# A mixture-of-experts product on TensorE: units of one expert by two token tiles become units of one token tile by two experts

## The chip, the core and the metric

The kernel runs on one core of a Trainium2 chip. The metric is the device time of one launch in microseconds; lower is better. Three runs of the kernel before gave 2796.57, 2797.51 and 2797.83 us, so the median is 2797.51 us.

## What is computed

Two transformer layers on x of shape 32 batches x 256 tokens x 256 features: cross attention, a mixture layer, a second attention without weights, and a sparse expert layer. The change touches only the mixture layer, which multiplies every token by all 12 experts, with a weight C that is zero for all but the three chosen ones:

```python
h = jax.nn.gelu(_mixture(xf, C1, W1), approximate=False)
y = _mixture(h, C2, W2) + C3 @ b2
# _mixture: for e in range(12): y = y + C[:, e:e + 1] * (inp @ W[e].T)
```

Every `inp @ W[e].T` is a 256x256 by 256x256 product for each batch; there are two mixtures (n = 0 with W1, n = 1 with W2), so 24 expert products in each of 32 batches, 768 in all.

## The kernel before, in words

All engines walk one list of pieces, `order`, that the function `pieces` sorts by hand-set places (the tables PLACES, MIX, OPENING and LAST at the head of the file). In the steady part a batch's work is spread over 40 places, and pieces of about five batches are interleaved: the attention of a later batch runs between the mixture products of an earlier one. Each engine takes from the list the pieces in which it has a part, in that order, and waits on semaphores only. Nothing is reordered at run time.

A mixture piece is `("mix", b, n, l)`, with b the batch, n the mixture and l from 0 to 11; its number is q = 24 b + 12 n + l. Tokens of a batch form two tiles t of 128 tokens; features form two blocks dt of 128.

- **TensorE** (`tensor_program`, line 1447). To keep fp32 accuracy with the fp32r type, each operand is split into a high and a low part, and a product is the sum of three terms (high by high, low by high, high by low), so 3 x 2 = 6 matmuls fill one output region. The stationary operand is a 128x128 block of tokens (`r_part`, `h_part` has the same memory), the moving one 128x256 of the expert's weights (`w_h`, `w_l`). The piece has 12 matmuls of 256 columns, six for each token tile, and fills one 512-column PSUM bank, `mixp[q % 2]`. Before it, TensorE waits until VectorE has done all adds of piece q - 2, which used the same bank. After it, `t_mix` goes up by one.
- **VectorE** (`vector_program`, line 1131; line 1125 for the first add of a tile in mixture 0). It waits for `t_mix` of the piece and does two adds, acc = psum * C + acc, of 128x256 elements: one for token tile 0, one for token tile 1. Each add waits through the semaphore `v_mix` for the add of the piece before that wrote the same tile. These two adds don't depend on each other.

Between mixture pieces TensorE does, among others: `first` (line 1347, attention scores whose row maxima VectorE takes at line 1039), `second` (1365, scores that ScalarE turns into exponentials at 854), `attn_out` (1381), transposes into the bank `misc` (1273, 1355, 1392), projections (1315, 1327, 1411), router products (1426, 1428, 1429), and the shared expert (1483, 1504, 1522). VectorE also does layer norm statistics (973 to 978, 1000), the attention's division (1057, 1062), splits into high and low parts (949, 954), `nmp` (1049, 1051) and the router's selection (1082 to 1111). The sparse experts run at the end, from about 2490 us, and have no mixture pieces.

Of the kernel before, what the change touches and what calls it, by code (L numbers as in the profile page):

```python
# [15 lines left out]
P = 128  # L16
# [234 lines left out]
def build(nc, x_in, ctx_in, ctxT_in, wqT_in, wkvT_in, woT_in, qk_cols_in, bv_cols_in, bo_in, pw_in, uT_in,  # L251
          w1T_in, w2T_in, b2_in, wgu_in, wd_in, wsgu_in, wsd_in, out_pad):
    NB, S, D = x_in.shape
    T = NB * S
    TILES = S // P
    DT = D // P
# [12 lines left out]
    NXB = 5  # L269
# [3 lines left out]
    TERMS = ((0, 0), (1, 0), (0, 1))  # L273
# [6 lines left out]
    with ctx:  # L280
# [9 lines left out]
        def sems(name, n):  # L290
# [18 lines left out]
        wmix = [[sb(f"w{n}_{p}", (P, L, DT, D), F32R) for p in "hl"] for n in (1, 2)]  # L309
# [13 lines left out]
        X = [x_mem[:, i] for i in range(NXB)]  # L323
        hid = sb("hid", (P, TILES, D))
# [36 lines left out]
        Cw = [sb(f"C{i}", (P, TILES, 3, L)) for i in range(2)]  # L361
# [51 lines left out]
        mixp, bank1, bank2 = ([mem[:, k, :] for k in range(2)] for mem in (mixp_mem, first, second))  # L413
# [47 lines left out]
        v_k, v_qt, v_q, v_ot, v_xo, v_rt, v_z, v_zd, v_C, v_mix, v_b2, v_ht, v_c3 = (  # L461
            sem(f"dve_{n}") for n in ("k", "qt", "q", "ot", "xo", "rt", "z", "zd", "C", "mix", "b2", "ht", "c3"))
# [454 lines left out]
        def vector_program(dve):  # L917
# [39 lines left out]
            for what, *a in order:  # L957
                if what == "w_mix":
                    split_lo(FIRST + a[0])
                elif what == "ln1":  # L960
                    kind, b = a
                    src = X[b % NXB]
# [16 lines left out]
                elif what == "ln2":  # L979
                    kind, b = a  # L980
                    src = X[b % NXB]
# [20 lines left out]
                elif what == "k_proj":  # L1002
                    b, = a
                    dve.wait_ge(a_k, 2 * (b + 1))
                    lo_biased(k_nat, 1, v_k)
                elif what == "c_done" and a[0] == NB - 1:
                    b, = a
# [4 lines left out]
                elif what == "q_proj":  # L1012
                    b, = a
                    dve.wait_ge(a_q, q_parts_of(job_J["A", b]))
                    lo_biased(q_nat, 0, v_q)
                elif what == "c_turn":
                    b, = a
                    dve.wait_ge(a_q, q_parts_of(job_J["C", b]))
                    lo(q_nat, v_q)
                elif what == "q_turn":  # L1020
                    b, = a
                    dve.wait_ge(a_qt, b + 1)
                    lo(a_parts, v_qt)
                elif what == "o_turn":
                    b, = a
                    dve.wait_ge(a_ot, b + 1)
                    lo(a_parts, v_ot)
                elif what == "r_turn":
                    b, = a
                    dve.wait_ge(a_rt, b + 1)  # L1030
                    lo(r_parts, v_rt)
                elif what == "h_turn":
                    b, = a
                    dve.wait_ge(a_ht, b + 1)
                    lo(h_parts, v_ht)
                elif what == "s1":
                    kind, b, J, h, u, j = a
# [5 lines left out]
                elif what == "max_rows":  # L1043
                    kind, b, J, h, u = a
# [8 lines left out]
                elif what == "out_turn":  # L1053
                    kind, b, J, h, u = a
# [10 lines left out]
                elif what == "o_proj":  # L1065
                    b, = a
# [3 lines left out]
                elif what == "r_z":  # L1070
                    b, = a
# [5 lines left out]
                elif what == "r_top":  # L1077
                    b, = a
# [34 lines left out]
                elif what == "mix":  # L1113
                    b, n, l = a
                    q = 2 * L * b + n * L + l
                    dve.wait_ge(t_mix, q + 1)
                    for t in range(TILES):
                        acc = (hid if n == 0 else X[b % NXB])[:, t, :]
                        src = mixp[q % 2][:, t * D:(t + 1) * D]
                        c = Cw[b % 2][:, t, n, l:l + 1]  # L1120
                        if n == 0 and l == 0:
                            dve.wait_ge(v_C, b + 1)
                            dve.wait_ge(t_ht, b)
                            dve.wait_ge(a_id, 1)
                            dve.e.tensor_scalar(acc, src, c, None, ALU.mult).then_inc(v_mix, 1)
                        else:
                            if l == 0:
                                dve.wait_ge(v_b2, 2 * b + t + 1)
                            else:
                                dve.wait_ge(v_mix, 2 * (q - 1) + t + 1)  # L1130
                            dve.e.scalar_tensor_tensor(acc, src, c, acc, ALU.mult, ALU.add).then_inc(v_mix, 1)  # L1131
                elif what == "b2":
                    b, = a
# [4 lines left out]
                elif what == "d_logits":  # L1138
                    b, = a
# [7 lines left out]
                elif what == "d_top":  # L1147
                    b, = a
# [29 lines left out]
                elif what == "d_pos":  # L1178
                    b, = a
# [21 lines left out]
                elif what == "d_up":  # L1201
                    b, = a
# [6 lines left out]
                elif what == "d_down":  # L1209
                    b, = a  # L1210
# [3 lines left out]
                elif what == "e_same":  # L1214
                    e, = a
# [18 lines left out]
                elif what == "e_gate":  # L1234
                    e, = a
# [4 lines left out]
                elif what == "e_down":  # L1240
                    e, = a
# [8 lines left out]
        def tensor_program(pe):  # L1250
# [26 lines left out]
            for dt in range(DT):  # L1277
                m = pe.e.matmul(misc[:, dt * 64:dt * 64 + 3 * L], pw[:, dt * P:(dt + 1) * P], uT[:, :], start=True,
                                stop=True)
# [3 lines left out]
            for dt in range(DT):  # L1283
                m = pe.e.matmul(mixp[0][0:2, 0:D], bv_cols[:, dt, :], stage[0][:, dt * D:(dt + 1) * D], start=(dt == 0),
                                stop=(dt == DT - 1))
            m.then_inc(t_bo, 1)
            pe.wait_ge(a_id, 1)
            for what, *a in order:
                if what == "q_turn":
                    b, = a  # L1290
# [3 lines left out]
                elif what == "c_turn":  # L1294
                    b, = a
# [3 lines left out]
                elif what in ("k_proj", "q_proj"):  # L1299
                    b, = a  # L1300
# [9 lines left out]
                    for c in range(2):  # L1310
                        out = misc[:, c * S:(c + 1) * S]
                        n = 0
                        for i, j in TERMS:
                            for dt in range(DT):
                                m = pe.e.matmul(out, w[j][:, dt, c * P:(c + 1) * P], x[i][:, dt, :], start=(n == 0),  # L1315
                                                stop=(n == 3 * DT - 1))
                                n += 1
                    m.then_inc(t_kp if isk else t_q, 1)
                elif what == "v_proj":
                    b, = a  # L1320
                    claim("misc", (a_v, b + 1))
                    for t in range(TILES):
                        out = misc[:, t * D:(t + 1) * D]
                        n = 0
                        for i, j in TERMS:
                            for dt in range(DT):
                                m = pe.e.matmul(out, ctx_parts[i][:, dt, t * P:(t + 1) * P], wkv[j][:, dt, D:2 * D],
                                                start=(n == 0), stop=(n == 3 * DT - 1))
                                n += 1
                    m.then_inc(t_vp, 1)  # L1330
                elif what == "s1":
                    kind, b, J, h, u, j = a
# [17 lines left out]
                elif what == "max_rows":  # L1350
                    kind, b, J, h, u = a
# [43 lines left out]
                elif what == "o_turn":  # L1395
                    b, = a
# [34 lines left out]
                elif what == "mix":  # L1431
# [8 lines left out]
                    else:  # L1440
                        pe.wait_ge(v_ht, b + 1)
                    src = r_parts if n == 0 else h_parts
                    for t in range(TILES):
                        k = 0
                        for i, j in TERMS:
                            for dt in range(DT):
                                m = pe.e.matmul(mixp[q % 2][:, t * D:(t + 1) * D], src[i][:, dt, t * P:(t + 1) * P],  # L1447
                                                wmix[n][j][:, l, dt, :], start=(k == 0), stop=(k == 3 * DT - 1))
                                k += 1
                    m.then_inc(t_mix, 1)  # L1450
                elif what == "c3":
                    b, = a
# [188 lines left out]
```

## Time and profile before

| | |
|---|---|
| median of three runs | 2797.51 us (2796.57 to 2797.83) |
| span of the profiled execution | 2796.0 us |
| TensorE matmul busy | 2627.6 us, 94% |
| TensorE weight loads busy | 2189.7 us, 78% |
| VectorE busy | 2229.3 us, 80% |
| ScalarE, GpSimd busy | 1074.1 us, 38%; 808.2 us, 29% |
| mean granted TensorE clock | 0.981 of 2.4 GHz |

The span is the time from the first to the last instruction of the one profiled execution; it is 1.5 us under the median of the runs, and no separate time of that execution was taken. Matmuls are pipelined: a matmul's recorded duration is longer than the distance to the next one's start, so the distance of starts is what a matmul costs in a row of them. Weight loads have a row of their own and overlap matmuls. In a timeline, consecutive instructions of one form are merged, with their count behind an x.

### The profile page before, as it was taken

The numbers are of one execution on the slowest core, as the hardware profiler recorded it, in microseconds if no ns is written. First come the engines' busy times: TensorE is split into PE (matmuls) and PEld (weight loads), VectorE is DVE, ScalarE is ACT, GpSimd is POOL, SyncE is SP. The second block draws the span as 40 slices with busy tenths as digits, with TensorE's granted clock in tenths as the row PEclk, the third lists the DMA queues.
The fourth block names the chain that finished last, engine by engine and source line by source line (L and its number), as shares of the span: only waits on it lengthen the run. The fifth ranks groups of instructions, "written<-read, shape, count | busy, mean of one in ns | idle before, by whom it ended". The sixth has DMA issues, their size and how long they took to land.

```text
span 2796.0 us, 59981 instructions
## 1 busy us (share of the span) xinstructions
PE 2627.6 (94%) x22949; PEld 2189.7 (78%) x22949; DVE 2229.3 (80%) x6135; ACT 1074.1 (38%) x1622; POOL 808.2 (29%) x829
## 2 busy tenths in 40 slices
PE   3899999999999999999999999999999999985999
PEld 2788788888888888888888888888888888763776
DVE  5678788888888888888888888888888888762554
ACT  3333334444434444433444444444443444322232
POOL 1000132322223222222222222322222232226444
PEclk9999999999999999999999999999999999986999
DMA  7644444444444434443444444343444343245997
GB/s 224 175 136 105 113 123 130 123 110 111 117 116 108 116 107 100 116 110 94 110 103 97 114 116 109 105 116 101 96 108 98 92 107 71 58 87 155 231 234 168
DMA packets 322210, 336.02 MB, mean 120 GB/s; under 512 B 46676, under 2 KB 302751, under 8 KB 321412
## 3 DMA queue, kind: packets, MB, share of 16 engines
q1 hardware_dynamic: 286404, 307.37, 42.4%
q0 software_dynamic: 33792, 18.52, 3.9%
q10 hardware_dynamic: 1728, 6.29, 0.7%
q8 instruction: 182, 2.98, 0.5%
q14 instruction: 104, 0.85, 0.1%
HBM read 191.65 MB, written 221.81 MB: 148 GB/s over the span
## 4 chain that ended last, share of the span: by engine, by line
PE 76%; DVE 17%; issue 3%; DMA 2%; POOL 1%; ACT 1%; SPq 1%; POOLq 0%; ACTq 0%; DVEq 0%
PE mixp L1447 34%; PE attn_out L1381 6%; DVE nm L1039 6%; PE first L1347 5%; PE second L1365 4%; DVE hid L1131 4%; PE misc L1315 3%; PE mixp L1549 3%; PE misc L1273 3%; PE misc L1483 2%; PE second L1568 2%; PE misc L1522 2%; PE misc L1392 2%; DVE xhat L1000 2%; PE first L1504 2%
## 5 line engine op out<-in xcount | busy, mean ns | idle before, releaser
L739 POOL DMA_INDIRECT expert_slots<-row_mem,sidx x512 | 507.2, 991 | 1065.1 <-PE first L1347 769.5
L854 ACT ACTIVATE exps<-second 128x1024 f32<-128x1024 f32 x512 | 525.7, 1027 | 735.8 <-PE second L1365 727.7
L1447 PE MATMUL mixp<-w_h,r_part_h 128*128 128x256 f32 x3072 | 666.8, 298 | 10.9 <-DVE hid L1131 6.1
L1039 DVE TENSOR_REDUCE nm<-first 128x4 f32<-128x1024 f32 x504 | 613.7, 1218 | 27.0 <-PE first L1347 23.6
L1447 PE MATMUL mixp<-w_h,r_part_l 128*128 128x256 f32 x3072 | 610.9, 280 | 0.0
L1447 PE MATMUL mixp<-w_l,r_part_h 128*128 128x256 f32 x3072 | 610.3, 280 | 0.0
L1447 PEld LDWEIGHTS mixp<-w_h,r_part_h 128*128 128x128 f32 x3072 | 469.0, 189 | 60.5 <-DVE hid L1131 22.2
L1447 PEld LDWEIGHTS mixp<-w_l,r_part_h 128*128 128x128 f32 x3072 | 469.7, 188 | 0.0
L1447 PEld LDWEIGHTS mixp<-w_h,r_part_l 128*128 128x128 f32 x3072 | 469.6, 188 | 0.0
L1131 DVE SCALAR_TENSOR_TENSOR x_mem<-mixp,C,x_mem 128x256 f32<-128x256 f32 x768 | 334.7, 477 | 75.4 <-PE mixp L1447 72.0
L1131 DVE SCALAR_TENSOR_TENSOR hid<-mixp,C,hid 128x256 f32<-128x256 f32 x704 | 301.5, 476 | 97.0 <-PE mixp L1447 96.8
L713 POOL TENSOR_TENSOR norm<-norm,minus_half 128x2 f32<-128x2 f32 x128 | 91.9, 718 | 699.9 <-DVE norm L978 699.9
L1381 PE MATMUL attn_out<-exps,vx 128*17 128x256 f32 x4096 | 273.7, 389 | 4.5 <-ACT exps L854 4.5
L1347 PE MATMUL first<-kst,qst 48*128 48x256 f32 x2016 | 235.8, 311 | 23.4 <-DMA qst<-q_parts 17.5
L1365 PE MATMUL second<-qst,kst 50*128 50x256 f32 x2048 | 234.9, 307 | 7.3 <-ACT exps L854 5.5
L1347 PEld LDWEIGHTS first<-kst,qst 48*128 48x128 f32 x2016 | 155.8, 188 | 75.4 <-issue 29.5
L1365 PEld LDWEIGHTS second<-qst,kst 50*128 50x128 f32 x2048 | 158.8, 189 | 61.3 <-issue 30.0
L1381 PEld LDWEIGHTS attn_out<-exps,vx 128*17 128x17 f32 x4096 | 95.2, 97 | 101.7 <-issue 24.7
L750 POOL DMA_INDIRECT out<-x_mem,sidx x64 | 99.0, 1547 | 113.6 <-DVE x_mem L1248 65.8
L861 ACT COPY out_sb<-attn_out 128x512 f32<-128x512 f32 x128 | 74.6, 583 | 101.0 <-PE attn_out L1381 98.2
L786 ACT ACTIVATE nat_h<-misc,qk_cols 128x256 fp32r<-128x256 f32 x128 | 53.7, 471 | 154.6 <-PE misc L1315 149.2
L1000 DVE TENSOR_SCALAR xhat<-x_mem,norm 128x256 f32<-128x256 f32 x192 | 93.7, 529 | 5.0 <-POOL norm L713 5.0
(236 smaller groups left out, 3585.9 us busy)
## 6 DMA issues: line engine op xcount, KB each, us to landing
kst<-k_parts SPq DMA_DIRECT2D x256, 192.0 KB, 4.0
qst<-q_parts SPq DMA_DIRECT2D x256, 192.0 KB, 4.5
q_parts<-nat_h SPq DMA_DIRECT2D x128, 256.0 KB
k_parts<-ctx_part_h SPq DMA_DIRECT2D x64, 256.0 KB, 2.5
k_parts<-nat_h SPq DMA_DIRECT2D x64, 256.0 KB, 5.6
q_parts<-nat_l SPq DMA_DIRECT2D x64, 256.0 KB
exps<-in_wgu SPq DMA_DIRECT2D x30, 384.0 KB, 4.0
expert_slots<-row_mem SPq DMA_DIRECT2D x16, 642.0 KB, 6.3
```

The lines of the kernel that those rows point to most:

```text
L713: pool.e.tensor_tensor(rstd[kind][:, :], veps[kind][:, :], minus_half[:, :], ALU.pow).then_inc(p_pow[kind], 1)
L739: pool.e.indirect_dma_start(out=slots_dram, out_offset=bass.IndirectOffsetOnAxis(ap=sidx[b % 2][:, t, k:k + 1], axis=0), in_=row[b % 2][:, ...
L750: pool.e.indirect_dma_start(out=out_pad, out_offset=bass.IndirectOffsetOnAxis(ap=eid[e % NID], axis=0), in_=ey[e % NY], in_offset=None, bo ...
L854: act.e.activation(exps[:, j % NU, :, :, :].rearrange("p k t s -> p (k t s)"), second[:, :, :].rearrange("p k s -> p (k s)"), ACT.Exp, sca ...
L1000: dve.e.tensor_scalar(dst[:, t, 0:D], src[:, t, :], mv[kind][:, t, 0:1], rstd[kind][:, t:t + 1], ALU.subtract, ALU.mult).then_inc(v_norm[k ...
L1039: dve.e.tensor_reduce(nm[u % 2][:, :, 2 * j:2 * j + 2].rearrange("p t k -> p k t"), (mixp_mem if in_mixp(b, kind, j) else first)[:, :, :]. ...
L1131: dve.e.scalar_tensor_tensor(acc, src, c, acc, ALU.mult, ALU.add).then_inc(v_mix, 1)
L1273: m = pe.e.transpose(v[:, dt, t * P:(t + 1) * P], src[:, t, dt * P:(dt + 1) * P], ident)
L1347: m = pe.e.matmul(bank[k][:, t * S:(t + 1) * S], q_st[u % 3][at, j, t * P:(t + 1) * P], k_st[u % 3][at, j, :], start=True, stop=True)
L1365: m = pe.e.matmul(bank2[k][:, s * S:(s + 1) * S], k_st[u % 3][at, j, s * P:(s + 1) * P], q_st[u % 3][at, j, :], start=True, stop=True)
L1381: m = pe.e.matmul(attn_out[r0:r0 + HD + 1, q * S:(q + 1) * S], vx[:, s, h * H // 2 + HQ * q + i, :], exps[:, (2 * q + i // 2) % NU, i % 2, ...
L1447: m = pe.e.matmul(mixp[q % 2][:, t * D:(t + 1) * D], src[i][:, dt, t * P:(t + 1) * P], wmix[n][j][:, l, dt, :], start=(k == 0), stop=(k == ...
```

## The change

The two experts 2i and 2i + 1 keep two pieces, but these divide the work the other way round. The piece with even l takes token tile 0 through both experts, the piece with odd l takes token tile 1 through both. On TensorE a piece is six matmuls; the moving operand is `wmix[n][j][:, e:e + 2, dt, :]`, two experts' 256 columns, 512 in all. On VectorE both adds of a piece write the same tile, and the second waits for the first. The list of pieces, the banks, and TensorE's waits stay.

```diff
--- before.py
+++ after.py
@@ -1114,20 +1114,24 @@
                     dve.wait_ge(t_mix, q + 1)
-                    for t in range(TILES):
-                        acc = (hid if n == 0 else X[b % NXB])[:, t, :]
-                        src = mixp[q % 2][:, t * D:(t + 1) * D]
-                        c = Cw[b % 2][:, t, n, l:l + 1]
-                        if n == 0 and l == 0:
+                    t = l % 2
+                    acc = (hid if n == 0 else X[b % NXB])[:, t, :]
+                    for i in range(2):
+                        e = l // 2 * 2 + i
+                        src = mixp[q % 2][:, i * D:(i + 1) * D]
+                        c = Cw[b % 2][:, t, n, e:e + 1]
+                        if n == 0 and e == 0:
                             dve.wait_ge(v_C, b + 1)
                             dve.wait_ge(t_ht, b)
                             dve.wait_ge(a_id, 1)
                             dve.e.tensor_scalar(acc, src, c, None, ALU.mult).then_inc(v_mix, 1)
                         else:
-                            if l == 0:
+                            if e == 0:
                                 dve.wait_ge(v_b2, 2 * b + t + 1)
+                            elif i:
+                                dve.wait_ge(v_mix, 2 * q + 1)
                             else:
-                                dve.wait_ge(v_mix, 2 * (q - 1) + t + 1)
+                                dve.wait_ge(v_mix, 2 * (q - 1))
                             dve.e.scalar_tensor_tensor(acc, src, c, acc, ALU.mult, ALU.add).then_inc(v_mix, 1)
@@ -1440,13 +1444,13 @@
                     src = r_parts if n == 0 else h_parts
-                    for t in range(TILES):
-                        k = 0
-                        for i, j in TERMS:
-                            for dt in range(DT):
-                                m = pe.e.matmul(mixp[q % 2][:, t * D:(t + 1) * D], src[i][:, dt, t * P:(t + 1) * P],
-                                                wmix[n][j][:, l, dt, :], start=(k == 0), stop=(k == 3 * DT - 1))
-                                k += 1
+                    e, t = l // 2 * 2, l % 2
+                    k = 0
+                    for i, j in TERMS:
+                        for dt in range(DT):
+                            m = pe.e.matmul(mixp[q % 2][:, 0:2 * D], src[i][:, dt, t * P:(t + 1) * P],
+                                            wmix[n][j][:, e:e + 2, dt, :], start=(k == 0), stop=(k == 3 * DT - 1))
+                            k += 1
                     m.then_inc(t_mix, 1)
```

## Rows read from the trace of the kernel before

**Rows 1.** The page: shares of the engines, chain by engine and line, two groups.
```profile
PE 2627.6 (94%) x22949; PEld 2189.7 (78%) x22949; DVE 2229.3 (80%) x6135; ACT 1074.1 (38%) x1622; POOL 808.2 (29%) x829
...
PE 76%; DVE 17%; issue 3%; DMA 2%; POOL 1%; ACT 1%; SPq 1%; POOLq 0%; ACTq 0%; DVEq 0%
PE mixp L1447 34%; PE attn_out L1381 6%; DVE nm L1039 6%; PE first L1347 5%; PE second L1365 4%; DVE hid L1131 4%; PE misc L1315 3%; PE mixp L1549 3%; PE misc L1273 3%; PE misc L1483 2%; PE second L1568 2%; PE misc L1522 2%; PE misc L1392 2%; DVE xhat L1000 2%; PE first L1504 2%
...
L1447 PE MATMUL mixp<-w_h,r_part_l 128*128 128x256 f32 x3072 | 610.9, 280 | 0.0
...
L1131 DVE SCALAR_TENSOR_TENSOR x_mem<-mixp,C,x_mem 128x256 f32<-128x256 f32 x768 | 334.7, 477 | 75.4 <-PE mixp L1447 72.0
```

**Rows 2.** Windows: one batch's period, and the steady part (stretch, length, busy us).
```profile
1006.60:1082.40 75.80, 74.24 (x687) 62.87 (x687) 65.60 (x180) 31.04 (x45) 21.91 (x23) 1.00 0.42 108
400.00:2200.00 1800.00, 1762.63 (x16308) 1492.53 (x16308) 1556.09 (x4236) 737.63 (x1046) 520.12 (x546) 1.00 0.43 109
```

**Rows 3.** Waits, 400 to 2200 us: us in total, times, longest us.
```profile
DVE hid L1131 <- PE mixp L1447: 72.9, 71, 1.9
...
DVE x_mem L1131 <- PE mixp L1447: 43.9, 96, 0.9
...
PE misc L1273 <- DVE ctx_o L1062: 11.9, 24, 0.5
```

**Rows 4.** The chain in order of time, 1000 to 1090 us (start, us, what).
```profile
1001.54 0.88 DVE hid L1131 x2
...
1006.59 0.53 DVE hid L1131 x2
...
1010.80 1.67 PE mixp L1447 x12
...
1027.55 0.88 DVE hid L1131 x2
...
1029.61 1.57 PE first L1504 x8
```

**Rows 5.** Timeline of TensorE, matmuls (start, us from first start to last end).
```profile
1003.30 0.40 PE L1447 MATMUL mixp<-w_h,r_part_h 128*128 128x256 f32 x2
...
1004.70 0.40 PE L1447 MATMUL mixp<-w_h,r_part_h 128*128 128x256 f32 x2
...
1039.51 0.28 PE L1355 MATMUL misc<-identr,nmp 128*16 128x128 f32 x2
```

**Rows 6.** Timeline of the sparse experts near 2652 us, and their groups by form.
```profile
2651.93 1.46 PE L1549 MATMUL mixp<-exps,xhat 128*128 128x384 f32 x4
...
2653.44 1.03 PE L1568 MATMUL second<-vx,router_mem 96*128 96x256 f32 x4
...
L1549 PE MATMUL mixp<-exps,xhat 128*128 128x384 f32 x120 | 43.7, 486 | 0.0
...
L1568 PE MATMUL second<-exps,router_mem 96*128 96x256 f32 x120 | 30.9, 379 | 0.0
```

**Rows 7.** Timeline: the first and the last of eight weight loads for the router.
```profile
1070.57 0.19 PEld L1426 LDWEIGHTS misc<-gT_both,r_part_h 128*128 128x128 f32 x1
...
1071.35 0.19 PEld L1429 LDWEIGHTS misc<-gT_both,r_part_h 128*128 128x128 f32 x1
```

**Rows 8.** Timeline of VectorE (start, us; in brackets idle before it and releaser).
```profile
1011.74 1.66 DVE L1131 SCALAR_TENSOR_TENSOR hid<-mixp,C,hid 128x256 f32<-128x256 f32 x4
...
1020.75 0.88 DVE L1131 SCALAR_TENSOR_TENSOR hid<-mixp,C,hid 128x256 f32<-128x256 f32 x2 [1.93 <-PE mixp L1447]
...
1039.19 0.18 DVE L1051 TENSOR_TENSOR nmp<-nm,nmp 128x16 fp32r<-128x16 f32 x1
...
1062.11 0.29 DVE L1193 TENSOR_TENSOR prep<-prep,pmask 128x128 f32<-128x128 f32 x1
1062.44 0.35 DVE L1196 MAX8 stop<-prep 128x8 f32<-128x64 f32 x2
...
1069.74 0.69 DVE L949 TENSOR_TENSOR r_part_l<-misc,r_part_h 128x512 fp32r<-128x512 f32 x1
```

## The prediction, written before the changed kernel was run

> **What bounds the kernel now.** I read the page first. TensorE is busy 94% of the span, VectorE 80%, and the chain that ended last is TensorE for 76% and VectorE for 17%; line 1447, the mixture, holds 34% of it alone [rows 1]. A share over the whole span hides stages, so I read windows next. In the steady part TensorE is busy 1762.6 of 1800 us; one batch takes 75.8 us, with 74.24 of TensorE and 65.60 of VectorE [rows 2]. So TensorE idles 1.56 us a batch and VectorE 10.2. The clock is at its upper level (1.00) there and plays no part. Then the waits: VectorE waits for mixture products 72.9 + 43.9 = 116.8 us over 24 batches, 4.9 us a batch; TensorE's waits for VectorE are short and regular, such as 0.5 us once a batch for `ctx_o` [rows 3]. Last the chain in order of time, which shows that a batch has two kinds of stretch. From 1001.5 to about 1015 us VectorE sets the pace: the chain runs through its adds and reaches TensorE at 1010.80 [rows 4]; it catches up only at 1020.75, where it waits 1.93 us [rows 8]. Outside that stretch TensorE is nearly always what is late, except for short visits such as the add at 1027.55 that leads to line 1504 at 1029.61 [rows 4].
>
> **TensorE's part.** The columns streamed stay the same; the number of matmuls and weight loads falls from 12 to 6 a piece. Two equal places of adjacent pieces start 1.40 us apart (1003.30, 1004.70) [rows 5], so a 256-column matmul costs 1.40 / 12 = 0.117 us. What would 512 columns cost? No fp32r matmul of that width is in the trace, so I bound it. Above: twice 0.117 = 0.235 us, and no gain. Below: the time of a weight load, since a load is still needed for each; where the moving operand has only 36 or 72 columns, eight loads start over 1071.35 - 1070.57 = 0.78 us, 0.111 us each [rows 7]. Between them I take the plain-fp32 rows. There 128 columns more cost 486 - 379 = 107 ns of duration, and a 256-column fp32r matmul lasts 280 ns, 99 less than a 256-column fp32 one [rows 1, 6]: fp32r streams a column in about half the time, so 512 fp32r columns weigh what 256 fp32 columns do. Four of those take 1.03 us, and with the last one's 0.379 us off the step is (1.03 - 0.379) / 3 = 0.217 us, with a weight load hidden behind each; the 384-column ones confirm it with (1.46 - 0.486) / 3 = 0.325 us, 0.108 more [rows 6]. So a piece costs 6 x 0.217 = 1.30 us in place of 1.41: **0.106 us less**, 0 at the upper bound, 0.74 at the lower. If the excess of a 256-column matmul over its streaming (117 - 107 = 10 ns) is paid once per matmul however wide it is, the step is 0.224 us and the gain 0.064.
>
> **VectorE's part.** It still does two adds a piece, of the same size. Before, neighbours are independent: four in a row take 1.66 us with 0.477 us for one [rows 1, 8], so they start (1.66 - 0.477) / 3 = 0.395 us apart and overlap by 0.08. After, the second add waits for the first. A dependent pair of neighbours in the trace is 1062.11 + 0.29 = 1062.40, next start 1062.44 [rows 8]: no overlap and a gap of 0.04. The second add then starts 0.477 + 0.035 = 0.51 us behind the first: **0.115 us more a piece**, 2.8 us a batch. Bounds: nothing, if the overlap survives; at the top the longer hand-off from VectorE to TensorE, 1039.19 + 0.18 = 1039.37 to 1039.51, 0.14 us [rows 5, 8], which makes 0.22. I take 0.115, as that row is the same engine waiting for itself. The Trainium skill speaks against charging this: "VectorE: DVE Perf Modes", section "The DRAIN you can't avoid", says that the next operation does not begin before the pipeline has emptied, and that a semaphore between two operations adds nothing. By that rule the charge is zero. The starts 0.395 us apart with durations of 0.477 do not agree with it.
>
> The other edits cost nothing. The first add of a piece now waits for all adds up to piece q - 2, not for the last piece's; those have left VectorE two instructions before. The waits on C, on the bias of the second mixture and TensorE's wait for piece q - 2 stay. Behind the new wait stands all of VectorE's queue: the row maxima (line 1039) that free bank `first`, the `ctx_o` and `nmp` steps that release transposes, and the adds that free `mixp`.
>
> **The sum.** Of 24 pieces a batch, I go along the stretches. In the VectorE-paced stretch the products of six pieces are not late, so their gain is lost, and six pieces' adds lie on the path: 6 x 0.115. The add before line 1504 is on the path [rows 4]. Two more hand-offs have almost no slack: `nmp` ends at 1039.37 and its transpose starts at 1039.51 [rows 5, 8], and `r_part_l` ends at 1070.43, with the router's first product at 1070.57 [rows 7, 8]; each has an add ahead of it. That makes 9 charged adds. A batch gains 18 x 0.106 - 9 x 0.115 = 1.91 - 1.04 = 0.87 us, 1.1%. The 24 steady batches count in full; the opening and closing eight, where other waits stand between, I count by half: 28 x 0.87 = **24 us**. The profiled span is 2796.0 and becomes 2772; the median of the runs is 1.5 us above the span, so 2773 us. VectorE will have 65.6 + 24 x 0.08 = 67.5 us busy in 74.9, 90%, and what is late next is VectorE.
>
> **The rivals.**
> *VectorE takes over (slower).* It adds 2.8 us a batch to an engine that already paces a fifth of it, while TensorE gets shorter by 2.5. Its place is the queue behind the second add; if more hand-offs tip over than I listed, gain is lost and charge added. With k pieces on VectorE's path both ways the change breaks even at 0.106 (24 - k) = 0.115 k, k = 11.5. With 18 it is +1.43 us a batch, 28 times 40 us: 2838. For it: the 10.2 us idle of VectorE are in large part real waits at fixed places, and two pieces of slack is all that `mixp` gives. Against: 1.93 us of idle at 1020.75 and 4.9 us a batch waiting for mixture products.
> *The matmul gains too little (no change).* With the step 0.224 the batch gains 18 x 0.064 - 1.04 = 0.11 us, 3 us in all: 2794. For it: 256 columns show such an excess; against: the wider rows of plain fp32 don't.
> *The dependent add is free.* Then 18 x 0.106 x 28 = 53 us: 2744. Against it stand the dependent rows.
> *The wide matmul runs at the pace of its weight load.* TensorE would lose 24 x 0.74 = 18 us a batch and VectorE be the floor: 65.6 + 2.8, and the 10.2 us of its idle without the 4.9 waiting for products, so 73.7 less what other waits for TensorE shrink, perhaps 2: some 71.7. Then 28 x 4.1 = 115 us: 2682. Against it: nothing in the trace streams fp32r at such a pace. The Trainium skill has a rule that points here: "TensorE: Matmul & The Clock Gate", section "Back-to-back issue gap", gives about 131 ns for each 512-column matmul in a sustained stream of load and matmul. No row here shows it; by it a piece would cost 0.79 us.
>
> **The numbers.** Chances: forecast 0.56, VectorE takes over 0.18, no change 0.14, free add 0.08, wide matmul at the load's pace 0.04. The likeliest gives 2773. The range runs from the free add at 2744, rounded to 2742, to half way into the case of VectorE taking over, 2812; it leaves out the cheap wide matmul and the far half of the slow case. About 0.2% (5.6 us) is what a measurement can tell from no change. Faster 0.66, same 0.14, slower 0.20.
>
> **What would show each step.** Right: line 1447 with about 4608 matmuls, six in a row 1.30 us from piece to piece; PEld busy down by about a quarter; the two adds 0.51 us apart, a merged pair 0.99 in place of 0.87; TensorE idle 1.5 to 3 us a batch, the chain's VectorE share above 17%, a batch of 74.9 us. Wrong: equal places of adjacent pieces still 1.40 apart (the wide matmul is no cheaper), pairs of adds still 0.87 (no charge), or TensorE idle above 3.5 us a batch with line 1447 waiting for line 1131 (VectorE has taken over).

## The result and the profile after

The changed kernel takes 2830.2 us (median of four runs, 2829.2 to 2830.8) where the kernel before takes 2797.7 us on the same chip: ratio 1.0115, 95% interval 1.0103 to 1.0127. It is 32 us slower; the forecast was 24 us faster. The profiled execution has a span of 2829.1 us. Among the runs of the experiments below one execution was far off, one of ten of `wide_indep_2` with 3228 us where the nine others took 2814 to 2821, and it is left out of that run's ratio.

The page of the changed kernel, shares, chain and the groups of the mixture (lines moved by four: 1447 is now 1451, 1131 is 1135):

```profile
PE 2622.5 (93%) x18341; PEld 1914.8 (68%) x18341; DVE 2292.6 (81%) x6135; ACT 1074.0 (38%) x1622; POOL 810.4 (29%) x829
...
PE 63%; DVE 28%; issue 4%; DMA 2%; ACT 2%; POOL 1%; SPq 1%; POOLq 0%; ACTq 0%; DVEq 0%
...
L1451 PE MATMUL mixp<-w_h,r_part_l 128*128 128x512 f32 x1536 | 484.6, 397 | 0.0
...
L1135 DVE SCALAR_TENSOR_TENSOR x_mem<-mixp,C,x_mem 128x256 f32<-128x256 f32 x768 | 369.4, 481 | 70.6 <-PE mixp L1451 52.0
```

Against [rows 1], 4608 matmuls and weight loads are gone and weight loads fall from 78% to 68%. TensorE's busy time hardly moves (2627.6 to 2622.5 us), and the chain's VectorE share grows from 17% to 28%. The product of 512 columns lasts 397 ns where one of 256 lasted 280.

Windows of the steady part (stretch, length, busy us of TensorE, weight loads, VectorE, ScalarE, GpSimd, clock, DMA), to be held against [rows 2]:

```profile
400.00:2200.00 1800.00, 1732.27 (x12682) 1269.76 (x12683) 1580.31 (x4174) 726.78 (x1031) 515.66 (x538) 1.00 0.43 108
```

The shared expert's products (line 1487, before 1483) come 76.9 us apart, batch after batch, where they came 75.8 apart before. Of these 76.9 us TensorE is busy 1732.27 / 1800 x 76.9 = 74.0 and idle 2.9; before it was 1762.63 / 1800 x 75.8 = 74.2 and 1.6 [rows 2]. So a batch costs 1.1 us more: 1.3 us more of idle TensorE, and 0.2 less of busy TensorE.

Timeline of TensorE in the changed kernel (start, us from first start to last end; in brackets idle before and releaser), against [rows 5]:

```profile
1019.68 0.73 PE L1451 MATMUL mixp<-w_h,r_part_h 128*128 128x512 f32 x2 [0.26 <-DVE hid L1135]
...
1021.18 0.63 PE L1451 MATMUL mixp<-w_h,r_part_h 128*128 128x512 f32 x2
1021.65 0.63 PE L1451 MATMUL mixp<-w_h,r_part_l 128*128 128x512 f32 x2
1022.12 0.63 PE L1451 MATMUL mixp<-w_l,r_part_h 128*128 128x512 f32 x2
1023.24 0.73 PE L1451 MATMUL mixp<-w_h,r_part_h 128*128 128x512 f32 x2 [0.49 <-DVE hid L1135]
```

Two wide matmuls start 0.467 us apart, so one costs 0.233 us and a piece 1.40 us. That is what twelve narrow ones took.

Timeline of VectorE in the changed kernel, against [rows 8]:

```profile
1018.63 1.91 DVE L1135 SCALAR_TENSOR_TENSOR hid<-mixp,C,hid 128x256 f32<-128x256 f32 x4
...
1027.77 0.99 DVE L1135 SCALAR_TENSOR_TENSOR hid<-mixp,C,hid 128x256 f32<-128x256 f32 x2
...
1033.67 1.00 DVE L1135 SCALAR_TENSOR_TENSOR hid<-mixp,C,hid 128x256 f32<-128x256 f32 x2 [1.91 <-PE mixp L1451]
```

Four adds take 1.91 us (before 1.66), a pair 0.99 to 1.00 (before 0.87). The second add starts 0.99 - 0.48 = 0.51 us behind the first. Four adds are 0.48 + 2 x 0.51 + 0.41, so from one piece to the next the adds still overlap, and the loss is in the second add alone.

The chain in order of time in the changed kernel (start, us, what), against [rows 4]:

```profile
1013.46 0.50 DVE hid L1127
...
1018.29 0.42 DVE ctx_o L1062
...
1024.68 0.89 DVE hid L1135 x2
...
1030.56 0.40 DVE hid L1135
...
1031.58 0.19 DVE nmp L1051
1031.77 0.14 issue
1031.90 0.28 PE misc L1359 x2
...
1050.00 1.22 DVE nm L1039
1051.21 0.40 DVE x_mem L1135
...
1052.24 0.19 DVE nmp L1051
1052.42 0.14 issue
1052.56 0.28 PE misc L1359 x2
```

Before, this path left VectorE at the product of 1010.80 [rows 4], some 9 us after it had come to it. Now it stays on VectorE from 1013.46 to 1031.77, 18 us without a break, and enters it again at 1050.00 for a hand-off (`nmp`) that was not on the path before.

Who waits in the steady part, 400 to 2200 us (us in total, times, longest), against [rows 3]:

```profile
PE mixp L1451 <- DVE hid L1135: 17.8, 48, 0.5
...
PE misc L1277 <- DVE ctx_o L1062: 15.2, 24, 0.6
...
PE first L1508 <- DVE nm L1039: 13.6, 24, 0.6
...
PE misc L1359 <- DVE nmp L1051: 11.3, 53, 0.8
...
PE first L1351 <- DVE nm L1039: 4.6, 23, 0.3
```

All five are TensorE waiting for VectorE, 62.5 us in sum. The kernel before has 32.1 us for the first four (5.3, 11.9, 10.7, 4.2) and none of the fifth. The difference is 30.4 us over 24 batches, 1.3 us a batch: all of TensorE's new idle time.

### The profile page after: what moved, and what is told of

It reads as the page before. It is cut to its first block, busy times and chain, and to the rows that moved or that the text cites. A ratio compares the mean times of both kernels' runs of the same rounds, so it can differ in the third digit from the quotient of the medians.

```text
span 2829.1 us, 50093 instructions
## 1 busy us (share of the span) xinstructions
PE 2622.5 (93%) x18341; PEld 1914.8 (68%) x18341; DVE 2292.6 (81%) x6135; ACT 1074.0 (38%) x1622; POOL 810.4 (29%) x829
## 4 chain that ended last, share of the span: by engine, by line
PE 63%; DVE 28%; issue 4%; DMA 2%; ACT 2%; POOL 1%; SPq 1%; POOLq 0%; ACTq 0%; DVEq 0%
PE mixp L1451 27%; DVE nm L1039 9%; DVE hid L1135 7%; PE attn_out L1385 4%; PE second L1369 4%; PE first L1351 4%; PE misc L1319 3%; PE mixp L1553 3%; PE misc L1487 2%; PE misc L1277 2%; PE second L1572 2%; PE misc L1396 2%; PE misc L1526 2%; DVE xhat L1000 2%; PE misc L1415 2%
## 5 line engine op out<-in xcount | busy, mean ns | idle before, releaser
L1451 PE MATMUL mixp<-w_h,r_part_h 128*128 128x512 f32 x1536 | 537.3, 431 | 22.7 <-DVE hid L1135 21.5
L1451 PE MATMUL mixp<-w_h,r_part_l 128*128 128x512 f32 x1536 | 484.6, 397 | 0.0
L1451 PE MATMUL mixp<-w_l,r_part_h 128*128 128x512 f32 x1536 | 482.5, 395 | 0.0
L1135 DVE SCALAR_TENSOR_TENSOR x_mem<-mixp,C,x_mem 128x256 f32<-128x256 f32 x768 | 369.4, 481 | 70.6 <-PE mixp L1451 52.0
L1135 DVE SCALAR_TENSOR_TENSOR hid<-mixp,C,hid 128x256 f32<-128x256 f32 x704 | 333.7, 481 | 88.7 <-PE mixp L1451 74.4
L1451 PEld LDWEIGHTS mixp<-w_l,r_part_h 128*128 128x128 f32 x1536 | 288.9, 188 | 70.7
L1451 PEld LDWEIGHTS mixp<-w_h,r_part_l 128*128 128x128 f32 x1536 | 289.3, 188 | 67.4
L1451 PEld LDWEIGHTS mixp<-w_h,r_part_h 128*128 128x128 f32 x1536 | 239.8, 189 | 88.1 <-DVE hid L1135 41.9
L1351 PEld LDWEIGHTS first<-kst,qst 48*128 48x128 f32 x2016 | 155.3, 188 | 116.2 <-issue 76.9
```

What stands on the lines that cost most here:

```text
L1351: m = pe.e.matmul(bank[k][:, t * S:(t + 1) * S], q_st[u % 3][at, j, t * P:(t + 1) * P], k_st[u % 3][at, j, :], start=True, stop=True)
L1451: m = pe.e.matmul(mixp[q % 2][:, 0:2 * D], src[i][:, dt, t * P:(t + 1) * P], wmix[n][j][:, e:e + 2, dt, :], start=(k == 0), stop=(k == 3 * ...
```

## Experiments

The kernels ran in six groups, each on one chip with the kernel before beside it; the result above is the first group. The chips differ: the kernel before took 2798 us in the first, fourth and last group, and 2824 to 2829 us in the three others, so only ratios and times from one chip are compared.

**Width and dependence, apart.** `wide_indep` keeps the six wide matmuls and brings back the two independent adds (a tile then gets products of the other tile's tokens):

```diff
-                        e = l // 2 * 2 + i
+                    for t in range(TILES):
+                        acc = (hid if n == 0 else X[b % NXB])[:, t, :]
...
-                                dve.wait_ge(v_mix, 2 * q + 1)
+                                dve.wait_ge(v_mix, 2 * (q - 1) + t + 1)
```

> The products of the changed kernel (six matmuls of 512 columns a piece) with the adds of the kernel before: the first half of a bank is added to tile 0 and the second to tile 1, and no add waits for its neighbour. The computation is changed: a tile receives products of the other tile's tokens, with the same number and size of operations. Theory A (a matmul costs its columns, so the width gives and takes nothing, and the whole loss is the dependent add): 2794 to 2801 us, 0.40 us between the two adds, pieces 1.40 us apart on TensorE. Theory B (the wide products do harm of their own, since fewer weight loads are hidden or a bank is held otherwise): 2805 us or more. Theory C (the dependent adds hide a gain of the products that would show on a free VectorE): under 2790 us.

`narrow_dep` does the reverse: the changed kernel's adds behind twelve matmuls of 256 columns.

```diff
+                    for h in range(2):
...
-                            m = pe.e.matmul(mixp[q % 2][:, 0:2 * D], src[i][:, dt, t * P:(t + 1) * P],
-                                            wmix[n][j][:, e:e + 2, dt, :], start=(k == 0), stop=(k == 3 * DT - 1))
+                                m = pe.e.matmul(mixp[q % 2][:, h * D:(h + 1) * D], src[i][:, dt, t * P:(t + 1) * P],
+                                                wmix[n][j][:, e + h, dt, :], start=(k == 0), stop=(k == 3 * DT - 1))
```

> The adds of the changed kernel (two experts to one tile, the second waits for the first) with 12 matmuls of 256 columns a piece as before; the computation is the reference's. Theory A: the whole loss is here, 2826 to 2834 us, the two adds 0.51 us apart. Theory B: only a part, 2805 to 2822 us. Theory C: slower than the changed kernel, over 2836 us.

Measured: 2819.6 and 2878.5 us beside 2829.3 for the kernel before, ratios 0.9968 (0.9955 to 0.9980) and 1.0173 (1.0156 to 1.0190). This chip ran everything slower than the first, and the changed kernel was not beside them. So all four corners were run on one chip.

> The kernel before, profiled on the same chip as the three others of this call, because the first call's chip took 2829 us for it and not 2798. Theory A and its rivals: ratio 1.000; a batch takes the time that the others are compared with.

> The changed kernel on the same chip. Ratio to the kernel before 1.010 to 1.014 as on the first chip. If the slower chip has its own share in the result, over 1.016.

> Dependent adds with narrow products again, beside the changed kernel on one chip. Theory A (the width does nothing): the changed kernel's time within 3 us. Theory D (with VectorE late, the six wide matmuls give something that twelve narrow ones don't): slower than the changed kernel by 8 us or more, and the profile shows in which wait.

> Wide products with independent adds again (tiles mixed up as in the first such run). Theory A: the time of the kernel before within 3 us. Theory D: 5 to 12 us faster than the kernel before.

| on one chip | independent adds | dependent adds |
|---|---|---|
| 12 matmuls of 256 columns | 2824.1 (before; 2823.7 over all its runs) | 2873.2, ratio 1.0181 (1.0164 to 1.0198) |
| 6 matmuls of 512 columns | 2818.2, ratio 0.9977 (0.9967 to 0.9987) | 2865.5 (changed), ratio 1.0149 (1.0132 to 1.0166) |

The dependent adds cost 49 us with narrow and 47 us with wide products. The wide products give 5.5 us and 7.7 us. Theory A is right about the loss and misses a small gain; theory D, which wanted it at 8 us under late adds and 5 to 12 under free ones, is met in the second place and just missed in the first. A batch takes 76.3, 76.1, 77.9 and 77.7 us (before, wide alone, dependent alone, both). The windows show what kind of gain it is, first the kernel before on this chip, then the wide products alone:

```profile
400.00:2200.00 1800.00, 1765.57 (x16204) 1487.02 (x16203) 1547.95 (x4211) 734.43 (x1041) 516.43 (x543) 1.00 0.43 109
```

```profile
400.00:2200.00 1800.00, 1764.42 (x12856) 1284.44 (x12852) 1551.99 (x4221) 736.13 (x1044) 517.63 (x544) 1.00 0.43 109
```

TensorE's busy time in a batch goes from 1765.57 / 1800 x 76.3 = 74.84 to 1764.42 / 1800 x 76.1 = 74.59 us: 0.25 us over 24 pieces, 10 ns a piece, a tenth of the 106 that the prediction counted.

**What a wide matmul costs.** Three runs of one execution each read the distance of the starts. `wide_384` multiplies 192 columns of each expert and leaves the others out:

```diff
-                            m = pe.e.matmul(mixp[q % 2][:, 0:2 * D], ...
-                                            wmix[n][j][:, e:e + 2, dt, :], ...
+                            m = pe.e.matmul(mixp[q % 2].rearrange("p (h d) -> p h d", h=2)[:, :, 0:192], ...
+                                            wmix[n][j][:, e:e + 2, dt, 0:192], ...
```

> The changed kernel with 2 x 192 columns a matmul (a quarter of each product left out), to read one number: the distance of the starts in a row of wide matmuls. Theory A (cost goes with the columns at 0.456 ns each, no fixed part): 0.175 us. A fixed part of 10 ns on 0.417 ns a column: 0.170 us. A step of 0.217 or more would mean a limit that the columns don't set.

> The changed kernel with the 512 moving columns read from one contiguous stretch (both feature blocks of one expert) and not from two stretches 512 elements apart; the products are then other ones than the layer's. Theory A: step 0.233 us as before. Rival (the jump between the two experts' weights costs the excess over 0.217): 0.217 us.

> The changed kernel with both operands of the mixture matmuls read as the upper two bytes of each element, in bf16; low parts of the split then carry less. If the 0.456 ns a column belong to reading fp32r: step 0.213 to 0.217 us. If it is TensorE's pace on this chip for any type: 0.233 us.

`wide_contig` replaces the moving operand by `wmix[n][j][:, l, :, :]`; `wide_bf16` reads both operands through `.bitcast(BF16)` with a step of two, the upper two bytes of each element. TensorE's timelines, 384 columns first, then contiguous, then bf16:

```profile
1010.79 0.51 PE L1451 MATMUL mixp<-w_h,r_part_l 128*128 128x384 f32 x2
1011.13 0.51 PE L1451 MATMUL mixp<-w_l,r_part_h 128*128 128x384 f32 x2
```

```profile
1010.41 0.63 PE L1451 MATMUL mixp<-w_h,r_part_h 128*128 128x512 f32 x2
1010.88 0.63 PE L1451 MATMUL mixp<-w_h,r_part_l 128*128 128x512 f32 x2
1011.34 0.63 PE L1451 MATMUL mixp<-w_l,r_part_h 128*128 128x512 f32 x2
```

```profile
1001.48 0.61 PE L1451 MATMUL mixp<-w_h,r_part_h 128*128 128x512 bf16 x2
1001.93 0.61 PE L1451 MATMUL mixp<-w_h,r_part_l 128*128 128x512 bf16 x2
1002.38 0.61 PE L1451 MATMUL mixp<-w_l,r_part_h 128*128 128x512 bf16 x2
1002.84 0.61 PE L1451 MATMUL mixp<-w_h,r_part_h 128*128 128x512 bf16 x2
...
1006.64 0.63 PE L1451 MATMUL mixp<-w_h,r_part_h 128*128 128x512 bf16 x2 [0.26 <-DVE hid L1135]
```

384 columns: the two rows shown start 0.34 us apart, 0.170 each, and over the whole steady part the median distance of neighbouring starts in the mixture is 0.175 us. 512 contiguous columns: 0.93 / 4 = 0.233, as with the jump between the experts. bf16: 1.36 / 6 = 0.227. So the jump costs nothing, and the cost follows the columns: medians of 0.117 us for 256, 0.175 for 384 and 0.234 for 512, 0.46 ns a column in all. A fixed 10 ns on top of 0.417 ns a column would give 0.224 for 512, which was not seen. The bf16 run answers neither side of its question: it removes 0.006 of the 0.020 us that lie between 0.233 and 512 columns at 2.4 GHz (0.213). Why a column takes about 9% longer than a cycle at that clock, with a granted clock of 1.00, stays open.

The bf16 run took 2798.5 us, where `wide_contig` took 2827.8 and the kernel before 2798.1 on that chip, and shortened the batch from 76.9 to 76.0 us. That can't be put down to the step alone. TensorE's busy time fell from 74.0 to 1714.48 / 1800 x 76.0 = 72.4 us a batch, by 1.6 us, where 24 x 6 x 0.006 is 0.9. The rows show another part: in the changed kernel the first pair of a piece that follows other work takes 0.73 us and a later pair 0.63 (1019.68 and 1021.18 above), in bf16 0.63 and 0.61. Weight loads are shorter too, 98 ns recorded in place of 188. Of the 1.6 us the batch got 0.9, and TensorE's five waits for VectorE grew from 62.5 to 81.8 us.

**Was only the step mis-sized?** With 238 columns of each expert, 18 of each product left out, the step is the 0.217 us that the prediction took.

> The changed kernel with 2 x 238 columns in each wide matmul, so 18 columns of each expert's product are left out, and VectorE's adds stay whole. Theory A (cost goes with the columns, 0.456 ns each): six matmuls take 1.30 us, which is the piece that the prediction counted on; with its count of 18 pieces gained and 9 adds charged the time is 2773 us, within 2766 to 2781. Rival 1 (VectorE holds more of the path once TensorE is shorter): 2795 us or more. Rival 2 (a fixed cost per matmul, so that fewer columns give less): six matmuls take over 1.35 us and the time is 2805 us or more.

> The same 2 x 238 columns, with the independent adds of the first experiment; 18 columns of each product are left out and the tiles are mixed up. By the prediction's count (18 pieces gained, no add charged) 2744 us, within 2736 to 2752. If VectorE holds more of the path than that count says, 2755 us or more; if less (all 24 pieces gain), 2732 us or less.

> 2 x 238 columns with dependent adds again (18 columns of each product left out), beside its twin on one chip; it gives the step of 0.217 us that the prediction counted on. If the prediction's only fault was the size of that step: ratio 0.991 (its 2773 us). If VectorE takes the gain, as the first such run said: 1.000 to 1.004.

> The twin with independent adds (18 columns left out, tiles mixed up): 0.984 to 0.987 as in the first such run, or, on a chip that runs the kernel before in 2797 us, where ScalarE's copy of the row maxima is not late, down to 0.981, which is the prediction's count of 18 pieces gained.

Measured, on two chips: 2836.6 and 2833.9 us with dependent adds, ratios 1.0025 (1.0015 to 1.0035) and 1.0019 (1.0009 to 1.0028); 2786.0 and 2785.6 us with independent ones, ratios 0.9846 (0.9829 to 0.9862) and 0.9851 (0.9830 to 0.9871). The timeline of `wide_476_3` has the step: starts at 1008.83, 1009.26 and 1009.70, 0.435 us for two, so 1.30 us a piece.

```profile
1008.83 0.59 PE L1451 MATMUL mixp<-w_h,r_part_h 128*128 128x476 f32 x2
1009.26 0.60 PE L1451 MATMUL mixp<-w_h,r_part_l 128*128 128x476 f32 x2
1009.70 0.60 PE L1451 MATMUL mixp<-w_l,r_part_h 128*128 128x476 f32 x2
```

So on these two chips even the step that was forecast does not make the change faster; the forecast's 2773 us would be a ratio of 0.991. A piece gives up 6 x (0.467 - 0.435) / 2 = 0.096 us of products, 24 of them 2.3 us. A batch of the steady part takes 76.9 us in place of 77.7 with dependent adds and 75.3 in place of 76.1 or 76.2 with independent ones, 0.8 to 0.9 us: 8 or 9 pieces' worth, not 18.

Over the whole time more comes: 2819.6 - 2786.0 = 34 us on the chip that ran `wide_indep` and `wide_476_indep`, where the prediction's way of counting, 18 x 0.096 x 28, gives 48. That is 12 to 13 pieces' worth, and a third of it lies outside the steady 24 batches. With dependent adds the ratio falls from 1.0149 to 1.0019 or 1.0025, some 35 us. Taken off the 2830 us of the first chip, these leave about 2795 us, no change, as an estimate; the run was not made there.

The waits of `wide_476_indep_3` show who took the rest:

```profile
PE misc L1327 <- ACT mT L848: 15.8, 24, 0.8
PE first L1504 <- DVE nm L1039: 10.5, 24, 0.4
PE mixp L1447 <- DVE hid L1131: 9.7, 23, 0.4
PE misc L1273 <- DVE ctx_o L1062: 5.6, 23, 0.3
PE second L1365 <- DMA qst<-mT: 5.2, 23, 0.8
```

With the wide products at full width on such a chip these five are 2.5, 10.5, 5.6, 3.1 and 1.1 us. Next to the adds it is ScalarE's copy of the row maxima and the transfer behind it that came last. On the first chip neither the kernel before nor the changed one has such a wait for the copy, so the count there may be better; that was not tried.

**Where the dependent add costs.** The new division in one mixture at a time (`if n == 0:` or `if n == 1:` around the new code, the old code in the other branch):

> Only mixture 0 (n = 0) is divided in the new way, mixture 1 stays as before; the computation is the reference's. The prediction's count charges 7 of its 9 adds here (six in the stretch that VectorE paces and the one before line 1504), so it expects 22 us over the kernel before, less 3 for the wide matmuls: ratio 1.006 to 1.009. If the charge is spread evenly over both mixtures (rival), half of the whole loss, 1.0055 to 1.0075, and the other half in mixture 1.

> Only mixture 1 is divided in the new way. By the prediction's count 2 adds are charged, 6 us, less 3 for the wide matmuls: ratio 1.000 to 1.002. If the charge is spread evenly: 1.0055 to 1.0075.

Measured beside 2828.9 us: 2861.9 and 2842.9 us, ratios 1.0122 (1.0102 to 1.0142) and 1.0049 (1.0035 to 1.0064). 33 and 14 us, in sum 47, close to the whole loss on such a chip (42). Mixture 0 holds 70% of it, where the paced stretch lies; both are above the count's 19 and 3 us.

What waits in mixture 1 is not what waited on the first chip. In `new_mix1`, from 400 to 2200 us, TensorE waits for VectorE as long as in the kernel before on such a chip (`before_again` has 5.3 us for `mixp`), and longer for ScalarE's copy of the row maxima:

```profile
PE misc L1348 <- ACT mT L848: 12.8, 22, 0.7
...
PE mixp L1477 <- DVE hid L1152: 5.0, 23, 0.2
```

The same copy grows with the whole change on the second chip, first the kernel before, then the changed kernel:

```profile
PE misc L1327 <- ACT mT L848: 2.4, 7, 0.6
```

```profile
PE misc L1331 <- ACT mT L848: 10.8, 19, 0.6
```

Mixture 1 costs 0.5 us a batch, 12 us over 24, and the wait for the copy is 10 us longer than in `before_again`; the kernel before was not profiled on the chip of `new_mix1` itself. On the first chip neither kernel has this wait. So part of what the slower chips lose beyond the 32 us of the first, 42 us on the second, goes through ScalarE's copy; what delays it there stays open.

**Relief in the paced stretch.** `norm_on_act` is the kernel before with the two normalisations of layer C on ScalarE, `after_norm` the changed kernel with the same edit:

```diff
+                    if kind == "C":
+                        dve.e.scalar_tensor_tensor(shift[:, :], mv[kind][:, :, 0], -1.0, rstd[kind][:, :], ALU.mult,
+                                                   ALU.mult).then_inc(v_ve["C"], 1)
+                        continue
...
+                    for t in range(TILES):
+                        act.e.activation(xhat[0][:, t, :], X[b % NXB][:, t, :], ACT.Identity, bias=shift[:, t:t + 1],
+                                         scale=rstd["C"][:, t:t + 1]).then_inc(v_norm["C"], 1)
```

> The kernel before, with one piece of VectorE's paced stretch moved: the two normalisations of layer C (1.42 us on the chain, 1003.4 to 1006) are done by ScalarE as scale and bias, and VectorE only computes the bias (0.17 us). The computation is the reference's. If VectorE paces that stretch, a batch loses 0.5 to 1.0 us and the ratio is 0.990 to 0.995. Rival (ScalarE is then late for its exponentials, or the stretch has another last wait): 0.998 or more.

> The changed kernel with the two normalisations of layer C moved to ScalarE. If what makes the changed kernel slow is VectorE being late in its paced stretch, relief there is worth more than in the kernel before, where it gave 7 us: 12 to 35 us under the changed kernel, ratio to the kernel before 1.001 to 1.010. If the dependent adds cost elsewhere, 7 us or less, ratio 1.009 to 1.013 on a chip like the first, 1.012 to 1.015 on one like the second.

> Its counterpart on the kernel before, again: ratio 0.996 to 0.9985.

Measured: 2790.8 and 2792.1 us, ratios 0.9974 (0.9965 to 0.9983) and 0.9978 (0.9968 to 0.9988) on the kernel before, 2813.4 us and 1.0056 (1.0042 to 1.0069) on the changed one. The same 1.25 us of VectorE's work is worth 6 to 7 us where the adds are independent and 32 - 15.5, some 17 us, where they are not. That is as it should be if VectorE's lateness in this stretch is what the changed kernel pays for. In the kernel before, 0.9974 lies outside the 0.990 to 0.995 that was hoped for, and next to the rival's 0.998, because the stretch has another last wait; the timeline of VectorE in `norm_on_act`, and TensorE's longest wait from 400 to 2200 us:

```profile
1001.66 0.15 DVE L1011 SCALAR_TENSOR_TENSOR shift<-norm 128x2 f32<-128x2 f32 x1
...
1005.65 0.87 DVE L1146 SCALAR_TENSOR_TENSOR hid<-mixp,C,hid 128x256 f32<-128x256 f32 x2
1007.40 0.75 DVE L986 BATCH_NORM_STATS2 norm<-x_mem 128x6 f32<-128x256 f32 x2 [0.89 <-POOL x_mem L728]
```

```profile
PE first L1362 <- DVE nm L1054: 13.5, 23, 0.7
```

VectorE is through its adds at 1006.52 and now stands 0.89 us for GpSimd's sum of layer C, which it used to find finished. TensorE's 11.9 us for `ctx_o` [rows 3] are gone, and 13.5 us for the row maxima have come, which the kernel before doesn't have at this line. `norm_on_act` leaves the computation as it is and is 6 to 7 us faster than the kernel before, so faster than both.

## Why the prediction was wrong

**The matmul's step failed, and it is the largest part of the miss.** The prediction bounded a 512-column fp32r matmul by 0.111 and 0.235 us, wrote that the upper bound is no gain, and chose 0.217 from the plain-fp32 rows. It is 0.233. The choice treated 99 ns and 107 ns as the same number [rows 1, 6]: the 8 ns by which 256 fp32r columns were dearer than half the fp32 price are most of the excess of 10 ns that it had found in the step of 0.117, and they double with the width. The nearest row was the matmul of the same type in the same line, and it said twice 0.117. Of 0.106 us a piece 0.010 came. In the prediction's sum that is 18 x 0.096 x 28 = 48 of the 57 us between 2773 and 2830. It is not the whole of it: `wide_476` has the forecast's step and was still 5 to 7 us slower than the kernel before. What it gave was some 35 us, and the other 20 or so stand in the two counts below. The prediction's own first sign of being wrong, equal places still 1.40 us apart, is what the trace shows.

**The dependent add was sized right.** The pair was to take 0.99 us and takes 0.99 to 1.00; the second add starts 0.51 us behind the first, as forecast. The rule of the Trainium skill that the prediction set against this charge ("VectorE: DVE Perf Modes", section "The DRAIN you can't avoid": a semaphore between two operations adds nothing) does not hold for these adds: independent ones start 0.395 us apart, dependent ones 0.51, and the latter cost 47 to 49 us. The same section adds that a next operation which is not held starts earlier. The prediction left that out, and the 0.395 us agree with it: the overlap is lost where the wait stands. Whether the wait itself or the common accumulator takes it away was not separated.

**The charged adds were too few, moderately.** Nine a batch made 1.04 us; TensorE's idle grew by 1.3 us on the first chip, and on the second the whole cost was 1.6 us a batch (77.9 against 76.3, or 77.7 against 76.1). Most of the list of places was right: `ctx_o`, the adds before line 1508, `mixp` and the `nmp` hand-off at 1052.56, whose slack was 0.14, all wait longer, and mixture 0 carries most. The router's hand-off was on the list and has no wait in either kernel. The paced stretch was too short in the list: the changed kernel's chain passes through the adds of eight pieces between 1013.46 and 1031.77, where the prediction had six, and of two more at 1040.47 and 1051.21. Ten times 0.115 is 1.15 us of the 1.3. The cost of mixture 1 on the slower chips stands in ScalarE's copy, which no term of the sum had.

**The gained pieces were too many.** The prediction subtracted six pieces for the paced stretch and let 18 gain. With its own step of 0.217 eight or nine gained in the steady part of the two chips tried, and 12 to 13 by the whole time. It took TensorE for late everywhere outside the stretch, on the strength of the chain, but with 2.3 us less work a batch TensorE runs up against the adds, ScalarE's copies and a transfer. With the right step this count hardly matters, since there is almost nothing to gain.

**The rivals and the range.** With the upper bound of the step and its own charge, 28 x 1.04 = 29 us, the sum gives 2827 us, 3 us off. That corner, no gain but full charge, was a bound in the text and no rival: the rival of no change kept a gain of 0.064 us, and the slow one put its cause in VectorE taking over more pieces with the products still cheaper. VectorE did take over in the sense that its chain share rose to 28%, though TensorE's idle time, 2.9 us a batch, stayed under the 3.5 that the prediction had named as the sign of it. The case was never weighed with the matmul at its upper bound, and the range, ended at 2812, left out a bound that it had itself named. That the sum with that bound comes so close is in part luck: on the second chip the dependent adds cost 47 to 49 us, not 29.

Three numbers of the prediction don't follow from its own. It took 1.41 us for a piece that its rows give as 1.40, so its gain a piece should have been 0.10 and not 0.106, 4 us in the sum. Half way into the slow case is not 2812: half way from 2773 to 2838 is 2806, from 2797.5 it is 2818. And its chances sum to 0.68 for faster and 0.18 for slower, not 0.66 and 0.20.

The rival of a wide matmul at the pace of its weight load is out. The rule cited beside it (the Trainium skill, "TensorE: Matmul & The Clock Gate", section "Back-to-back issue gap", about 131 ns for 512 columns in a stream) fits no run here: 233 ns in fp32r and 227 in bf16, each with a weight load and at a granted clock of 1.00.

## What to carry to other kernels

Halving the number of matmuls at the same count of columns buys nothing where the step of a matmul already goes with its columns: divide the step by the width for the same type before pricing a new width, and keep the factor of two as the first guess. Two VectorE operations that depend on each other cost their full duration plus a gap, here 0.51 us and not 0.40, so an order that alternates between two accumulators is worth keeping even when both adds of one bank would be convenient together. When an engine idles 13% but paces one stretch, count what a change does there, and put both bounds of an unmeasured price through the whole sum before the range is closed.

## What the runs showed of the hardware that was not expected

- fp32r columns cost 0.46 ns each from 256 to 512 columns, at a granted clock of 1.00, contiguous or not; bf16 columns read with a step of two cost 0.443 ns. Neither is a column a cycle at 2.4 GHz (0.417 ns).
- A weight load behind each matmul cost next to nothing at 256 columns: halving the number of matmuls and loads took TensorE's busy time down by 10 ns a piece.
- The first pair of fp32r matmuls behind other work takes 0.1 us more than a later pair, in bf16 0.02 or nothing. The change could not save it, as it is paid once for a row of matmuls.
- The same kernel takes 2798 us on three chips and 2824 to 2829 us on three others. On a slower one a batch takes 76.3 and not 75.8 us, and TensorE waits at line 1327 for ScalarE's `mT`, which on the first chip it does not. The changed kernel lost more there, 42 us against 32, and waits for `mT` 10.8 us where the kernel before waits 2.4. Why the chips differ stays open.
